# A wavelet block on one core: in the last 21 tiles, x is added to the second channel half by an accumulating DMA

## What is computed

```
ll, lh, hl, hh = haar_dwt(x)
wav   = concatenate([ll, lh, hl, hh], axis=1)                  # 1024 channels, 80 x 80
fused = relu(bn1(conv1x1(wav, fusion_w, fusion_b)))            # 256 channels
sp_map      = conv7x7([mean over channels, max over channels of fused])
spatial_out = sigmoid(sp_map) * fused
ch_map      = sigmoid(mlp(avg over pixels) + mlp(max over pixels))
projected   = relu(bn2(conv1x1(ch_map * spatial_out, proj_w, proj_b)))   # 1024 channels
out   = haar_idwt(projected split in 4) + x
```

## Time and profile before

| | |
|---|---|
| median of 3 runs | 2507.8 us (2505.55 to 2510.87) |
| profiled execution, its own time | 2504.5 us |
| its span, first to last instruction | 2502.4 us |
| busy: PE, DVE, ACT, POOL | 93%, 88%, 43%, 15% |
| mean granted TensorE clock | 0.982 of full speed |

### The profile page before, as it was taken

The page is one execution under the profiler, slowest core; times in us unless marked ns, Lnnn a source line. Parts: engine busy times, 40 slices in busy tenths (PEclk is TensorE's granted clock), DMA queues, the critical chain, the costliest instruction groups (busy, mean ns, idle before and its releaser), DMA issues. The chain is left out here.

```text
span 2502.4 us, 30155 instructions
## 1 busy us (share of the span) xinstructions
PE 2328.4 (93%) x11109; PEld 2046.7 (82%) x11109; DVE 2191.4 (88%) x2844; ACT 1072.3 (43%) x1413; POOL 387.6 (15%) x345
## 2 busy tenths in 40 slices
PE   5999899999999999998999999999999999976886
PEld 4787789897888889887898878988898888955765
DVE  4877888898889988898888988899888998888998
ACT  2445544354344544454443544445434554323222
POOL 0010111111111111111111111111111111122333
PEclk8999999999999999999999999999999999988999
DMA  3455699998999999999999999999999999986687
GB/s 133 167 173 195 184 286 287 279 303 256 281 291 275 282 270 279 277 296 261 280 288 283 290 256 281 290 272 292 256 281 290 283 291 258 250 289 244 244 285 280
DMA packets 112615, 660.54 MB, mean 264 GB/s; under 512 B 17682, under 2 KB 18772, under 8 KB 112212
## 3 DMA queue, kind: packets, MB, share of 16 engines
q1 hardware_dynamic: 86260, 488.21, 51.3%
q0 software_dynamic: 26208, 170.41, 36.9%
HBM read 448.24 MB, written 210.33 MB: 263 GB/s over the span
## 5 line engine op out<-in xcount | busy, mean ns | idle before, releaser
L493 PE MATMUL pp<-y_hi,wp_hi 128*128 128x480 f32 (+1 forms) x1792 | 678.0, 378 | 81.3 <-DVE y_lo L816 43.2
L507 PE MATMUL pf<-x_hi,wf_hi 128*128 128x480 f32 (+1 forms) x1792 | 672.7, 375 | 33.4 <-DVE x_lo L736 14.4
L493 PE MATMUL pp<-y_lo,wp_hi 128*128 128x480 f32 (+1 forms) x1792 | 670.4, 374 | 0.0
L493 PE MATMUL pp<-y_hi,wp_lo 128*128 128x480 f32 (+1 forms) x1792 | 668.9, 373 | 0.0
L507 PE MATMUL pf<-x_hi,wf_lo 128*128 128x480 f32 (+1 forms) x1792 | 668.4, 373 | 0.0
L507 PE MATMUL pf<-x_lo,wf_hi 128*128 128x480 f32 (+1 forms) x1792 | 668.2, 373 | 0.0
L571 ACT ACTIVATE x_hi<-xin 128x1920 fp32r<-128x1920 f32 (+1 forms) x224 | 419.8, 1875 | 544.7 <-PE pf L507 536.7
L736 DVE TENSOR_TENSOR x_lo<-xin,x_hi 128x1920 fp32r<-128x1920 f32 (+1 forms) x224 | 461.5, 2061 | 192.6 <-ACT x_hi L571 192.4
L601 ACT ACTIVATE relu<-pp,t 128x480 f32<-128x480 f32 (+1 forms) x448 | 284.3, 642 | 413.5 <-PE pp L493 369.1
L493 PEld LDWEIGHTS pp<-y_hi,wp_hi 128*128 128x128 f32 x1792 | 341.1, 190 | 142.2 <-DVE y_lo L816 59.1
L793 DVE SCALAR_TENSOR_TENSOR xre<-sd,both 128x960 f32<-128x960 f32 (+1 forms) x364 | 410.2, 1169 | 6.5
(11 more groups left out here) (89 smaller groups left out, 1169.8 us busy)
## 6 DMA issues: line engine op xcount, KB each, us to landing
xin<-in_x_dram SPq DMA_DIRECT2D x160, 960.0 KB, 7.6
out_dram<-xre SPq DMA_DIRECT2D x160, 960.0 KB, 5.9
xre<-in_x_dram POOLq DMA_DIRECT2D x130, 960.0 KB, 9.5
xin<-in_x_dram SPq DMA_DIRECT2D x64, 800.0 KB, 7.5
out_dram<-xre SPq DMA_DIRECT2D x64, 800.0 KB, 5.4
xre<-in_x_dram POOLq DMA_DIRECT2D x52, 800.0 KB, 9.5
xre<-in_x_dram SPq DMA_DIRECT2D x30, 960.0 KB, 6.6
sigb<-sig_scratch SPq DMA_DIRECT2D x56, 400.0 KB, 7.9
```

Source lines behind the costliest of these rows:

```text
L493: mm = pe.matmul(pp[j][:, 0:n_px], w[:, kt, cols], y[:, s.pc, kt, 0:n_px], start=(kt == 0 and m == 0), stop=(kt == CT - 1 and m == 2))
L507: mm = pe.matmul(pf[o][:, 0:n_px].rearrange("p (y w) -> p y w", w=W2), w[:, i, q, o * P:(o + 1) * P], v[:, q % 2, :, q // 2, :], start=(i ...
```

## The change

For i = 1, `adding` is now always true. So in the tail the second channel half of each tile is no longer loaded by SP and added by DVE and GpSimd; its cells go straight into the `xre` buffer, GpSimd issues an accumulating DMA, and SP stores when that has landed. The first half stays as it was. Nothing changes ahead of the tail.

```
         def adding(kc, i):
-            return kc + LAG < NT
+            return i == 1 or kc + LAG < NT
...
             for s in slots:
                 body(s)
-            residual(gp, nc.gpsimd, NT - 1, 1, 1, added_p)
+            add_x(NT - 1, 1)
...
             for s in slots[1:]:
                 body(s)
-            residual(dve, nc.vector, NT - 1, 1, 0, added_v)
```

## The result

| | before | changed |
|---|---|---|
| median | 2509.3 us (4 runs, 2505.6 to 2511.9) | 2539.9 us (4 runs, 2530.1 to 2546.2) |
| ratio, 95% interval | | 1.0123 (1.0091 to 1.0155) |
| profiled execution: time, span | 2504.5, 2502.4 us | 2530.1, 2528.3 us |

What follows compares the result with a forecast made beforehand. DVE was taken to pace the tail, then a chain through a shared buffer: 12.2 + 4.8 - 5.7 + 4.4 = 15.7 us on 2507.8 gave 2523.5 us (chance 0.54), own range 2517 to 2533, all cases 2503 to 2540.

Steps and rivals of the forecast that it cites:

- +12.2 us: Slots 120 to 132: the chain through the shared buffer outlasts today's slots, 9 x 0.76 + 4 x 1.33 us slower in all.
- cells, 2.35 us: First leg of the 6-row chain in the tail: DVE's cells of the second half take 2.35 us.
- the rival of the DMA engines: Tail: all 16 DMA engines set the pace, 16.0 us per 6-row slot, +32 us, 2540 us; chance 0.19.
- load, "I take 7.9": Leg of the 6-row chain: SP's load of a first half beside accumulating DMAs takes 7.9 us.
- Store, "I take 5.8": Leg of the 6-row chain: SP's store of half 1 takes 5.8 us, as a second store follows directly.
- Accumulating DMA, "10.7": Leg of the 6-row chain: the accumulating DMA, with a store and a load beside it, takes 10.7 us.
- 28.5 us for a pair of 6-row slots: Tail: sum of the chain's legs, closing after two slots, 14.25 us per slot against 13.49 before.
- The chain's path: Tail: cells, accumulating DMA, store, load into the same buffer after that store, addition, cells; 28.5 us per two 6-row slots.
- Gate, "+4.8": Slots 113 and 114: the first multiplication by the spatial map starts 4.8 us later, behind a later load and map store.
- Savings, "-5.7": Slots 115 to 119: DVE paces and keeps the saved additions, three of 1.24 and two of about 1.0 us.
- End, "+4.4": After the last cells: an accumulating DMA and a store make 11.0 us in place of 6.6, 4.4 us more.
- The rival "DVE keeps the pace": Tail: chain below 24.5 us, DVE sets 12.25 us per 6-row slot, about -15 us, 2493 us; chance 0.13.

## Why the prediction was wrong

The direction was right, and so was the loop that the prediction named. What failed is the size of the term for slots 120 to 132, "+12.2 us", measured 22.9. The step in it that failed is the leg "cells, 2.35 us": the sum had no term for what GpSimd's share of the additions that stay would do to DVE once x is late. That 2539.9 us is still inside the range over all cases, 2503 to 2540, is luck: its upper end comes from the rival of the DMA engines, which did not hold. By its own steps:

- *"cells, 2.35 us"*: 4.30 in a late slot. I had looked at GpSimd's additions only for whether DVE waited for them. Before, they ran beside the butterflies, which read PSUM; a late x moved them beside the cells. Leaving them out gave back 8.2 of the 10.7 us that the term was short by.
- *load, "I take 7.9"*: 11.0 to 11.7 in three of the four 6-row loops of the chain, 9.7 in the other. The other loop's accumulating DMA and a second store ran beside it (in the loop shown issued at 2369.79 and 2368.1, the load at 2371.46). *Store, "I take 5.8"*: 3.7, although the second store followed 0.4 us behind it, which was my reason for 5.8. Why it was so quick the runs do not show. *Accumulating DMA, "10.7"*: 10.2 to 10.8 in the late half of the loop. In the loop shown, load and store together are 14.7 against my 13.7. The two errors partly cancelled.
- 28.5 us for a pair of 6-row slots became 30.7; the mean over the 8 slots from 2352.84 to 2471.84 is 14.9 us. DVE's rows add up: 168.0 before, less 15.4 for the additions saved (9 x 1.24 + 4 x 1.07), plus 25.4 of waiting for x, 11.1 of longer cells in six late slots and 2.5 more of waiting for TensorE, is 191.6 against 190.9.
- *The chain's path*: I put it through the buffer, with SP's order as a side effect. In the changed kernel both close the loop at the same point. With own buffers the loop stayed, and with the load also ahead of the stores it was gone. Either tie alone is enough to keep it. The buffer alone would have been a story that fits the trace.
- *Gate, "+4.8"*: +7.4. I had the later issue, 1.7 us (measured 1.8), but not that the 25 KB store would land only with the load ahead of it, after 11.2 us and not 5.0.
- *Savings, "-5.7"*: -6.0. *End, "+4.4"*: +5.3, with 7.6 for the DMA, 3.3 for the store, and 1 us more.
- *The rival "the DMA engines are the limit"*: its number, 2540 us, is the one that was measured, but not by its mechanism. At a share of 0.84 the same transfers could still be done 18% faster; with both halves by DMA the engines are the limit.
- *The rival "DVE keeps the pace"*: it needed legs shorter than 24.5 us. With plain writes they were, and the kernel was 12 us faster than before.

"Waits of 1 to 3 us in most slots" was wrong as well: it was 4.3 to 5.5 us in five of the six late slots and 0.9 in the other, and a late slot is every second one, since only one of the two interleaved loops is late at a time.

## What to carry to other kernels

A loop through several queues has to be listed with each queue's order, not only with its buffers: here, once the buffers were separate, one load behind one waiting store still cost 28 us. Separate buffers alone gave 3 us, and the move is possible only with them. When a step becomes late, ask what it will then run beside. Cheap work that was hidden under one instruction can land on another that it disturbs.

## What the runs showed of the hardware

- Two DVE instructions with both tensor inputs in SBUF (the cells) took 4.29 us beside a GpSimd addition and 2.35 alone. DVE instructions with one input in PSUM (the butterflies) took 0.70 to 0.72 us with or without the same addition beside them. The Trainium skill, "SBUF — State Buffer", section "Who interferes with whom", says that a DVE instruction with two SBUF inputs contends with a GpSimd instruction that reads SBUF; these traces agree for the cells. DVE's own addition L291, also with two inputs in SBUF, took 1.16 us beside GpSimd's, started 0.1 us ahead of it, and 1.15 alone; there it was GpSimd's that grew, from 2.26 to 3.11.
- An accumulating DMA costs the 16 engines 5.0 to 5.4 us per MB and a plain one 2.5 to 2.8 in every window read here.
- A 25 KB store that was issued on SP behind a 960 KB load landed within 0.3 us of that load: 11.2 us after its issue when the load took 11.4 with an accumulating DMA under way, 8.1 and 5.0 when the load took 8.4 and 7.0 without one and was 0.5 and 2.2 us ahead.
